# Masking the turned scores of causal attention with TensorE products instead of a GpSimd selection

## What is computed

```
def _dense_path(x, wq, wk, wv, wo, w1, w2, w3, attn_norm_w, ff_norm_w):
    ...
    scores = jnp.einsum('bqhd,bkhd->bhqk', q, k) / np.sqrt(hd)      # hd = 8, 16 heads, 4 batches, 512 tokens
    causal = jnp.tril(jnp.ones((s, s), bool))
    scores = jnp.where(causal, scores, jnp.finfo(scores.dtype).min)
    attn = jax.nn.softmax(scores, axis=-1)
    o = jnp.einsum('bhqk,bkhd->bqhd', attn, v).reshape(b, s, d)
    h = x + rmsnorm(o @ wo, attn_norm_w)
    ...
```

## Time and profile before

| | |
|---|---|
| runs of the kernel | 1222.74, 1223.06 and 1227.17 us, median 1223.06 |
| the profiled execution | 1220.72 us, its span 1219.0 us |
| mean granted TensorE clock | 0.967 |
| TensorE busy | 1099.5 us, 90% of the span |
| VectorE, ScalarE, GpSimd busy | 804.8, 740.8 and 340.4 us |
| GpSimd's selections (L906) | 128, from 175.8 to 327.7 us |
| turned scores of the causal stage (L992) | 256 products, from 174.0 to 326.9 us |

### The profile page before, as it was taken

The page is one execution under the profiler, slowest core; times in us unless marked ns, Lnnn a source line. Parts: engine busy times, 40 slices in busy tenths (PEclk is TensorE's granted clock), DMA queues, the critical chain, the costliest instruction groups (busy, mean ns, idle before and its releaser), DMA issues. The chain is left out here.

```text
span 1219.0 us, 35588 instructions
## 1 busy us (share of the span) xinstructions
PE 1099.5 (90%) x14750; PEld 560.9 (46%) x14750; DVE 804.8 (66%) x1312; ACT 740.8 (61%) x1464; POOL 340.4 (28%) x668
## 2 busy tenths in 40 slices
PE   6999888888899998689999999999978887899996
PEld 2344443333234443456767666766645334222221
DVE  4897558777623233267767676776735557999984
ACT  5314627777544434366776676776745374899994
POOL 0552203333225344144324233322204332100000
PEclk9999959999989999799999999999999998999999
DMA  5000144111063300431120120110010003511100
GB/s 198 1 0 1 27 130 147 54 43 30 5 138 70 69 1 0 138 40 10 11 16 8 11 18 8 10 10 8 8 11 1 1 0 88 191 55 44 43 17 35
DMA packets 134495, 51.61 MB, mean 42 GB/s; under 512 B 103920, under 2 KB 126464, under 8 KB 133696
## 3 DMA queue, kind: packets, MB, share of 16 engines
q1 hardware_dynamic: 134300, 49.32, 17.3%
q10 hardware_dynamic: 36, 0.02, 0.0%
HBM read 33.09 MB, written 15.81 MB: 40 GB/s over the span
## 5 line engine op out<-in xcount | busy, mean ns | idle before, releaser
L2379 DVE TENSOR_REDUCE re_nmax<-ps 128x1 f32<-128x512 f32 x256 | 158.9, 683 | 88.9 <-PE ps L2147 88.9
L2290 ACT ACTIVATE normed<-ps,re_nmax 128x512 f32<-128x512 f32 x256 | 158.9, 688 | 89.8 <-DVE re_nmax L2379 89.8
L2168 PE MATMUL ps<-const,normed 128*128 128x128 f32 x1024 | 145.9, 282 | 7.7 <-ACT normed L2290 4.8
L1200 DVE TENSOR_REDUCE ga_nmax<-ps 128x2 f32<-128x1024 f32 x128 | 146.9, 1215 | 4.2 <-PE ps L956 4.1
L1104 ACT ACTIVATE ga_pt<-ps 128x512 f32<-128x512 f32 x256 | 139.2, 598 | 15.2 <-PE ps L992 14.2
L2168 PEld LDWEIGHTS ps<-const,normed 128*128 128x128 f32 x1024 | 108.7, 141 | 38.1 <-ACT normed L2290 28.0
L1200 DVE TENSOR_REDUCE da_nmax<-ps 128x2 f32<-128x256 f32 (+3 forms) x128 | 102.4, 821 | 35.3 <-PE ps L967 34.3
L1104 ACT ACTIVATE da_pt<-ps 128x512 f32<-128x512 f32 (+3 forms) x256 | 96.9, 435 | 43.3 <-PE ps L992 41.1
L1630 DVE TENSOR_TENSOR ex_u<-ps,ex_s 128x512 f32<-128x512 f32 x48 | 32.8, 690 | 99.4 <-PE ps L1495 76.5
L2296 ACT ACTIVATE re_pT<-ps 128x512 f32<-128x512 f32 x128 | 76.4, 597 | 28.0 <-PE ps L2168 19.6
L2399 DVE COPY re_pT<-ps 128x512 f32<-128x512 f32 x128 | 82.2, 683 | 9.8 <-PE ps L2168 9.0
(11 more groups left out here) (397 smaller groups left out, 1984.6 us busy)
## 6 DMA issues: line engine op xcount, KB each, us to landing
ex_gates<-gates_scratch SPq DMA_DIRECT2D x4, 2048.0 KB, 14.7
da_qst<-da_stacks SPq DMA_DIRECT2D x32, 96.0 KB, 2.2
da_kst<-da_stacks SPq DMA_DIRECT2D x32, 96.0 KB, 2.3
ga_qst<-ga_stacks SPq DMA_DIRECT2D x32, 96.0 KB
ga_kst<-ga_stacks SPq DMA_DIRECT2D x32, 96.0 KB
da_stacks<-da_qkparts SPq DMA_DIRECT2D x6, 384.0 KB, 3.2
ga_stacks<-ga_qkparts SPq DMA_DIRECT2D x6, 384.0 KB, 2.7
weights<-in_weights SPq DMA_DIRECT2D x1, 2048.0 KB, 8.0
```

Source lines behind the costliest of these rows:

```text
L1200: nc.vector.tensor_reduce(nmax[:, u % 2, :, pr, qt], g.ps[:, 2 * (step % S_GROUPS):2 * (step % S_GROUPS) + 2, 0:keys_of(qt)], AX.X, ALU.ma ...
L2168: last = nc.tensor.transpose(g.ps[:, bank_of("tile", s, idx), bass.ts(kt, 128)], p[:, QUAD_ORDER[idx], bass.ts(kt, 128)], g.c("ident"))
L2290: nc.scalar.activation(p[:, QUAD_ORDER[idx], :], g.ps[:, S_BANK + QUAD_ORDER[idx], :], ACT.Exp, bias=nmax[:, s % 2, idx:idx + 1]).then_inc ...
L2379: nc.vector.tensor_reduce(nmax[:, s % 2, idx:idx + 1], g.ps[:, S_BANK + quad, :], AX.X, ALU.max, negate=True).then_inc(maxed, 1)
```

## The change

The turned scores get their mask in PSUM, before the exponentials. Behind the two products L992, `scores_t` issues two more, one on each bank: the bf16 identity as weights (128x128) against `loweredT_bf` (128 columns), added onto the square on the diagonal. `st_scored`, for which the exponentials wait, is now raised by the second of them. The exponential of such a sum is zero. GpSimd's loop and the semaphore `selected` are gone, and the values wait for the exponentials directly.

```diff
@@ gpsimd @@
                     if front:
                         front.gpsimd(pool)
-                    if causal:
-                        for t in range(STEPS):
-                            u, r = divmod(t, 8)
-                            kt, pr = divmod(r, 2)
-                            q0 = first_query(kt)
-                            pool.wait_ge(exped, 2 * t + 2)
-                            square = pt[:, (4 * u + kt) % SLOTS, 2 * pr:2 * pr + 2, q0:q0 + 128]
-                            nc.gpsimd.affine_select(square, square, [[0, 2], [1, 128]], ALU.is_ge, 0.0, base=0,
-                                                    channel_multiplier=-1).then_inc(selected, 1)
                     if finish:
                         finish.add(pool)
@@ tensor, scores_t @@
                             last = nc.tensor.matmul(g.ps[:, st_bank(st_slot[t, par]), q0:T],
                                                     kst[rows, u % NBUF, pr, bass.ts(kt, 128)],
-                                                    qst[rows, u % NBUF, pr, q0:T], start=True, stop=True)
+                                                    qst[rows, u % NBUF, pr, q0:T], start=True, stop=not causal)
+                        if causal:
+                            for par in range(2):
+                                last = nc.tensor.matmul(g.ps[:, st_bank(st_slot[t, par]), q0:q0 + 128], g.ident_bf[:, :],
+                                                        g.loweredT_bf[:, :], start=False, stop=True)
                         last.then_inc(st_scored, 1)
@@ tensor, values @@
-                        if causal:
-                            pe.wait_ge(selected, 8 * u + 2 * kt + 2)
-                        else:
-                            pe.wait_ge(exped, 2 * (8 * u + 2 * kt + 2))
+                        pe.wait_ge(exped, 2 * (8 * u + 2 * kt + 2))
```

More of the change, by code:

```diff
@@ L784, in attention_stage @@
             (one, ones_set, zeroed, scored, maxed, split1, split2, split3, split4, m_turned, m_ready,
-             st_scored, exped, selected, o_cleared, pv_done, o_out) = (sem(n) for n in (
+             st_scored, exped, o_cleared, pv_done, o_out) = (sem(n) for n in (
                  "one", "ones_set", "zeroed", "scored", "maxed", "split1", "split2", "split3", "split4",
-                 "m_turned", "m_ready", "st_scored", "exped", "selected", "o_cleared", "pv_done", "o_out"))
+                 "m_turned", "m_ready", "st_scored", "exped", "o_cleared", "pv_done", "o_out"))
             DIRECT = 2
```

## The result

| | before | changed |
|---|---|---|
| median | 1225.12 us (4 runs, 1222.74 to 1228.88) | 1240.77 us (4 runs, 1239.29 to 1242.22) |
| ratio | | 1.0127, 95% interval 1.0098 to 1.0157 |
| forecast | | 1238.0, range 1230 to 1245 |
| one round of the causal stage | 9.27 us | 10.13 us (forecast 9.27 + 0.86) |

The change costs 15.7 us, by the interval 12 to 19. The page of the changed kernel shows where the engines' time went: GpSimd has 287.3 us in place of 340.4, the 53 us of its selections, and TensorE 1128.9 in place of 1099.5.

The account below looks back on a forecast made before the run. A ring through TensorE, ScalarE and the maxima's DMA bounds the causal stage: 15 passages at 0.86 us (12.9), 0.7 for half clock, 0.64 and some 0.7 at the end, less 0.1, give +14.8 on 1223.1: 1238 us, range 1230 to 1245.

Parts of the forecast that it names:

- The ring: Causal stage: dependent chain through TensorE, ScalarE and the maxima's DMA sets each eight-step round at 9.27 us; masks add 0.86.
- the first rival: Each causal step: weights loaded ahead make the mask's second array-shape change free; 0.66 us a round, 1234 us, chance 0.11.
- step 2: Second of a round's eight steps: turned scores 0.22 late plus mask's 0.21, both counting, exponential 0.43 us late.
- The rival with a free second change: Same as the first rival: no cost for the second array-shape change, 0.12 us a step on TensorE, chance 0.11.
- The covered steps: A round's last three steps, in the maxima DMA's shadow: masks add 0.66 against 0.76 us of waiting, barely covered.
- The ends: Causal stage's start and end: 0.7 us extra at half clock, 0.64 and some 0.7 after the last maxima, less 0.1.
- the first passage: First of 15 times round the ring, at half clock: five uncovered steps at 0.32, 1.6 us in place of 0.86.
- the masks that fit into idle time: Rival, causal rounds: masks fill TensorE's waits, 1.16 us idle a round; 1223 to 1227 us, chance 0.08.
- the faster kernel: Rival, before a round's first values: without selections the output copy moves forward, up to 0.6 us a round; 1213.5 us, chance 0.05.

## Why the prediction was right

- **What bounds.** The ring was read from one round of the timeline, and it held in every kernel with masks: a mask costs where it stands in a link (10.13 us with four of eight steps masked) and nothing elsewhere (9.27).
- **What is removed.** Expected 0 in the ring, measured 0 from both sides (10.13 with and without the selections, 9.27 with and without). The argument that counted was the 0.01 us between the ends of the selection and of the output copy; the row of waits, 9.6 us for GpSimd, would have misled. I took 0.1 us for the end of the stage, and nothing speaks for it or against it.
- **What is added, a step.** 0.22 us on TensorE, measured 0.22: 0.06 between the masks (I took 0.07), 0.15 from the second mask to the next product, a stream of 0.055 and a change of shape of 0.095. The rule by which weight loads are pulled ahead over such a change (the first rival) was tested by taking the change away: 0.11 us a round in the one step where it could show. The change of shape is paid, and the weights are not ahead: their load starts with the product, at 250.24, while that of L969, in the shape of the products before it, starts at 244.61, 0.22 us ahead of its own. The rule of the Trainium skill that a change of tiling mode drains the engine ("TensorEngine Tiling (Array Packing)", section "Key Properties") agrees with this row; the rule of the pull-ahead, which its page ties to conditions, does not reach over such a change here.
- **What lies on the ring.** 0.86 forecast, 0.86 to 0.87 measured, split 0.64 and 0.22 as worked out. But that split hid a mistake of reasoning that two equal numbers covered. In step 2 I added TensorE's 0.22 and the exponential's 0.21; the masks in pieces show that three times the exponential's lateness, through the ring of three banks, comes to the same (0.63), and that less of TensorE's time there wins nothing. The rival with a free second change was therefore priced too low: 0.75 a round and not 0.66.
- **The covered steps.** Here the reasoning was wrong and the outcome lucky. I took TensorE's two waits, 0.50 for VectorE and 0.26 for the DMA, as 0.76 us of room, and expected 0.10 of it to remain after 0.66. But the maxima that TensorE waits for come later when its own masks of the scores do, so the wait for VectorE is not room. Measured, the room was 0.42 us, L947 came 0.39 later against the DMA's issue, and 0.03 remained. The same error made me expect up to 0.7 us from the second DMA on GpSimd, which gave 0.43.
- **The ends.** From the stage's start to its end the trace has 198.0 us before and 213.0 after, 15.0 more against 14.8 forecast. 2.1 lie before the first output copy, a part of them at half clock, 13.0 in the 15 rounds between the first and the last copy, and nothing behind the last. I had 1.6 for the first passage, at half clock, and 1.3 for what stands behind the last maxima. The half clock at the stage's start lasted 27.3 us both times.
- **The total.** 15.7 us between the medians. I had put the forecast on a median of 1223.06, and before now has 1225.12, so 1238 was 2.8 low, of which 2.1 is this. That the rest is under 1 us is partly luck: the interval of the difference is 7 us wide. The two rivals without a loss, the masks that fit into idle time and the faster kernel, fell with the rounds.

## What to carry to other kernels

Work on an idle engine can be free, and a wait that the profile books on it can be free too: look at what else ends at the same moment before counting it as a gain. Find the ring that sets a round, by following one link to the next until the same instruction comes again, and ask of each added instruction whether it stands in a link; half of these masks cost everything and the other half nothing. A product in another shape of the array than its neighbours costs two changes of about 0.1 us, more than its own stream, and where an engine waits on the product, its lateness comes back through the banks, so that a shorter time of TensorE alone may win nothing. An engine's wait inside a covered stretch is room only if what it waits for does not itself wait for that engine.

## What was not expected

- Two rings of nearly equal length, 9.27 and 8.84 us. One edit shortens a round by 0.2 us, another by 0.43, and both together by no more than 0.2 in most rounds, because a split on VectorE and a selection on GpSimd start at the same moment; and where rounds were 0.2 to 0.4 us shorter, the medians stayed within 0.15% of before.
- Single rounds of 10.2 to 11.1 us among even ones of 9.38, 9.49 or 8.84, in three of the kernels. All five follow a late landing of the maxima or the half clock behind it: with the mask in step 5 alone the turned scores came 3.19 us after the issue (in pieces 3.52) in place of 2.70, and behind each of these, as in the rows shown with the DMA on GpSimd, the granted clock was at its lower level for 3.4 to 6.8 us. What held the DMA was not tried.
